# The last stage of a decoder on one core: norms in two VectorE passes, no GpSimd, weights prepared one stage earlier

## The chip, the cores and the metric

The kernel runs on 1 core of one Trainium2 chip. The metric is device time in microseconds (us) of one execution. The kernel before takes 4188.58 us, the median of 3 runs (4187.02 to 4195.04).

## The reference, cut to what matters

The network is a two-layer decoder: a recurrent mixer, cross attention, a mixture of experts, four selective-scan layers, an attention over feature maps, and at the end a quantised feed-forward network. Each sublayer is added to its input and layer-normalised. There are 4 batches of 512 tokens with 256 channels. Only the last sublayer is computed differently by the change:

```python
def act_quant_fake(x):
    scale = 127.0 / jnp.clip(jnp.max(jnp.abs(x), axis=-1, keepdims=True), 1e-05)
    return jnp.clip(jnp.round(x * scale), -128.0, 127.0) / scale
def weight_quant_fake(w):
    scale = 1.0 / jnp.clip(jnp.mean(jnp.abs(w)), 1e-05)
    return jnp.clip(jnp.round(w * scale), -1.0, 1.0) / scale
def bitlinear(x, w, b):
    return jnp.einsum('btd,hd->bth', act_quant_fake(x), weight_quant_fake(w)) + b
h = layernorm(x, ln1_g, ln1_b)        # 256 channels
h = bitlinear(h, w1, b1)              # 256 -> 1024
h = jax.nn.gelu(h, approximate=False)
h = layernorm(h, ln2_g, ln2_b)        # 1024 channels
h = bitlinear(h, w2, b2)              # 1024 -> 256
x = _layernorm(x + h)                 # what the kernel writes out
```

## The kernel before

The activations `x` stay in SBUF for the whole run as 128 partitions x 16 tiles x 256 channels; a batch is 4 tiles of 128 tokens (`TPB` = 4). Each sublayer is a stage of its own, a block with one written instruction stream for each engine, and a stage begins when all streams of the one before have ended. Inside a stage the engines are ordered by hand: a `Steps` object names the operations of one engine in their order, each completion adds one to a semaphore, and `wait_ge(*steps.at(name, turn))` holds an engine until that operation of that batch is done.

The last two compute stages are `feature_attention` (L2257) and `quantised_ffn` (L2536); `write_out` (L2846) follows.

**Attention stage.** Eight units `u` for each batch (4 tiles x 2 halves of the heads). TensorE makes scores, VectorE takes the row maximum (L2444), subtracts it (L2448), sums (L2438) and inverts (L2440) after ScalarE's exponential (L2369); GpSimd multiplies (L2327); TensorE transposes, ScalarE copies out (L2366); then come two products and, one batch later, the residual and norm. `head(b)` on VectorE (L2404) makes the block-diagonal operands from what ScalarE wrote in `projected(b)` (L2348).

**Quantised stage.** SyncE issues eight loads (L2585, L2589). VectorE sums the magnitudes of both weights (L2753), TensorE adds over partitions (L2787), VectorE scales and rounds the first weight in two passes (L2763, L2765), GpSimd the second (L2650, L2652), and ScalarE casts both to bf16 (L2598). Rounding is done by adding and taking away 1.5 * 2^23. For one batch of 4 tiles the chain is:

- first norm on VectorE: statistics (L221, L225, L228), ScalarE's root (L242), reciprocal (L233), subtract and multiply (L236), gain (L2696), offset (L2698);
- `quantise` on VectorE (L2663): maximum (L2669), three small operations (L2672, L2674, L2676), multiply and clip (L2679), clip and add the rounding constant (L2682), inverse scale (L2684); ScalarE takes the constant away into bf16 (L2607);
- TensorE transposes (L2795), ScalarE copies (L2610), TensorE multiplies into four PSUM banks (L2803), VectorE evacuates with scale and bias (L2708), ScalarE does the gelu (L2614);
- second norm over 1024 channels: statistics (L2715, L2719, L2722), root (L2618), reciprocal (L2726), subtract and multiply (L2729), gain (L2732) on VectorE, offset on GpSimd (L2657); then `quantise` again, ScalarE's cast (L2624), transposes (L2811), copies (L2628), the second product (L2817), and on VectorE the residual (L2741), the bias (L2745) and the last norm (L221 to L236 once more).

The order on VectorE is written by hand, with the first half of batch b+1 drawn between the parts of batch b:

```python
with v.Fori(0, B - 1) as b:
    first_stats(b + 1)
    second_norm(b)
    first_quantised(b + 1)
    second_quantised(b)
    first_products(b + 1)
    second_stats(b + 1)
    second_products(b)
```

`h2`, the hidden activations, has one buffer for all batches. `Fori` is a loop in the instruction stream with a register. The output leaves in one DMA of 2 MB after the last batch (L2852).

Of the kernel before, what the change touches and what calls it, by code (L numbers as in the profile page):

```python
# [2257 lines left out]
def feature_attention(nc, g, m):  # L2258
# [9 lines left out]
    with ExitStack() as ctx:  # L2268
# [31 lines left out]
        with nc.Block() as block:  # L2300
            @block.sync
            def _(sp):
# [5 lines left out]
                for dst, src in loads:  # L2308
                    sp.dma_start(dst, src).then_inc(weights_in, 16)
            n_loads = 16 * 6  # L2310
# [27 lines left out]
            def _(a):  # L2338
                begin(a, act_h, act_u, act_t)
# [56 lines left out]
            def _(v):  # L2396
                begin(v, dve_h, dve_u, dve_t)
# [35 lines left out]
                def body(b, tail=True):  # L2433
# [7 lines left out]
                    for u in us:  # L2441
# [9 lines left out]
                        if tail and u == 1:  # L2451
                            finish(b - 1)
                    sums(UN - 1)

                head(0)
                body(0, tail=False)
# [6 lines left out]
            def _(t):  # L2463
                begin(t, pe_h, pe_u, pe_t)
# [20 lines left out]
                def body(b, following=True):  # L2485
# [10 lines left out]
                    for u in us:  # L2496
# [6 lines left out]
                        if u >= LAG:  # L2503
                            at(u - LAG)
                        if following and u == 3:
                            transposes(b + 1)
                        if following and u == 7:
                            projections(b + 1)
# [17 lines left out]
                with t.Fori(0, B - 1) as b:  # L2526
                    body(b)
# [5 lines left out]
QUANT = " ".join(f"q{n}" for n in ["max", "clip", "rec", "scale"] + [f"{n}{q}" for n in ("mul", "low") for q in range(TPB)] + ["inv"])  # L2533


def quantised_ffn(nc, g, m):  # L2536
# [4 lines left out]
    HF = 1024  # L2541
    FC = HF // P
    with ExitStack() as ctx:
        sb, pb, sem = memory(nc, ctx)
        w1, w2 = sb("qf_w1", [P, DC, HF]), sb("qf_w2", [P, FC, D])
        wq1, wq2 = sb("qf_wq1", [P, DC, HF], BF16), sb("qf_wq2", [P, FC, D], BF16)
        wsum, wmean, wscale = sb("qf_wsum", [P, 2]), sb("qf_wmean", [P, 2]), sb("qf_wscale", [P, 2])
        identb = sb("qf_identb", [P, P], BF16)
        neground = sb("qf_neground", [P, 1])
# [4 lines left out]
        h2 = sb("qf_h2", [P, TPB, HF])  # L2554
        h2q = sb("qf_h2q", [P, TPB, HF], BF16)
        h2T = sb("qf_h2T", [P, TPB, FC, P], BF16)
# [6 lines left out]
        norm_in, w1_in, w2_in, rows_in = (sem(f"qf_{n}") for n in ("norm_in", "w1_in", "w2_in", "rows_in"))  # L2563

        ws, ws_g = Steps(sem("qf_weights_vector"), "ident sum mean clip rec r1 l1"), Steps(sem("qf_weights_pool"), "r2 l2")
        ws_a, ws_p = Steps(sem("qf_weights_scalar"), "q1 q2"), Steps(sem("qf_weights_tensor"), "sum")
        tl = range(TPB)
        each = lambda name: " ".join(f"{name}{q}" for q in tl)
        signal = lambda name, steps: Steps(sem(f"qf_{name}"), steps, 2)
        pre = lambda p, names: " ".join(p + n[2:] for n in names.split())  # L2570
        quant = lambda p: " ".join(p + n for n in QUANT.split())
        pe1, pe2 = signal("tensor_1", "h1T " + each("h")), signal("tensor_2", "h2T0 " + " ".join(f"h2T{q + 1} o{q}" for q in tl[:-1]) + f" o{TPB - 1}")
        act1, act2 = signal("scalar_1", "ansqrt q h1T " + each("g")), signal("scalar_2", "bnsqrt " + each("q") + " " + each("h2T") + " cnsqrt")
        dve1 = signal("vector_1", pre("an", LN_VECTOR) + " g1 b1n " + quant("a") + " " + each("e"))
        dve_st = signal("vector_stats", "bnstats bnmean bneps")
        dve2 = signal("vector_2", "bnrstd " + each("bnout") + " " + each("g2_") + " " + quant("b") + " res b2 " + pre("cn", LN_VECTOR))
# [3 lines left out]
        with nc.Block() as block:  # L2580
# [12 lines left out]
            def _(a):  # L2593
# [39 lines left out]
                for q in tl:  # L2633
                    gelu(0, q)
# [248 lines left out]
```

## Time and profile before

| what | value |
|---|---|
| median of 3 runs | 4188.58 us |
| the profiled execution, its own time | 4183.34 us |
| its span | 4181.5 us |
| busy in the span: TensorE, VectorE, ScalarE, GpSimd | 75%, 71%, 45%, 47% |
| chain that ended last | ends with the output DMA, then the last batch's norm |

The span is the time from the first to the last recorded instruction or transfer; the execution's own time has 1.84 us around it. The busy shares are means over all stages, and the change touches only what lies behind 3690 us, where the attention stage begins. Times in the profile are counted from the span's start. A timeline row gives the start, the busy time, the engine, the line, the operation, output and input, the count of instructions, and in brackets the idle time before them with what ended it. Rows of one kind that follow each other are merged.

### The profile page before, as it was taken

How to read it: one execution, taken by the hardware profiler on the slowest of the kernel's cores; microseconds unless marked ns; L12 is line 12 of the kernel's file. 1: busy time of each engine (PE TensorE's matmuls, PEld its weight loads, DVE VectorE, ACT ScalarE, POOL GpSimd, SP SyncE). 2: the span in 40 equal slices, each digit the busy share in tenths (PEclk: the TensorE clock that was granted, in tenths of full speed). 3: DMA queues.
4: the chain of work that ended last, by engine and by line, in shares of the span. 5: the costliest groups of instructions: out<-in, count | busy, mean ns of one | idle time of the engine just before them, and what ended most of it. 6: DMA issues, size and time to landing. Idle time of an engine off the chain costs nothing. (4 is left out here: it accounts for less than half of the span.)

```text
span 4181.5 us, 47419 instructions
## 1 busy us (share of the span) xinstructions
PE 3127.2 (75%) x16134; PEld 1728.5 (41%) x16134; DVE 2984.3 (71%) x3959; ACT 1885.0 (45%) x2885; POOL 1982.9 (47%) x1001
## 2 busy tenths in 40 slices
PE   6785888884664984788888988888998888657322
PEld 2234787774343751333333433333443333234111
DVE  2434666667541112899999999999999999946697
ACT  2323333321320113666667766666776666324232
POOL 0001111111213012678888878888878888722212
PEclk8775777776877996899999999999999999979665
DMA  1000000000021323343443444344444434300100
GB/s 39 0 0 6 0 0 0 0 0 5 18 87 60 114 89 103 111 149 137 156 144 132 148 138 157 133 147 142 153 139 139 146 134 141 131 13 0 39 0 20
DMA packets 120508, 342.10 MB, mean 82 GB/s; under 512 B 14667, under 2 KB 45602, under 8 KB 119618
## 3 DMA queue, kind: packets, MB, share of 16 engines
q1 hardware_dynamic: 114498, 332.01, 23.4%
q0 software_dynamic: 3072, 6.00, 0.7%
q10 hardware_dynamic: 2816, 2.62, 0.2%
q8 instruction: 57, 0.93, 0.1%
q14 instruction: 65, 0.53, 0.0%
HBM read 328.31 MB, written 14.68 MB: 82 GB/s over the span
## 5 line engine op out<-in xcount | busy, mean ns | idle before, releaser
L1916 POOL TENSOR_TENSOR mb_h<-mb_h,mb_BC 128x1024 f32<-128x1024 f32 x512 | 1212.2, 2384 | 362.1 <-DVE mb_h L2129 362.1
L2232 PE MATMUL mb_y<-mb_h,ident 128*128 128x512 f32 x2048 | 1027.6, 644 | 232.6 <-POOL mb_h L1916 231.1
L2129 DVE TENSOR_TENSOR_SCAN mb_h<-mb_dA,mb_bx 128x1024 f32<-128x1024 f32 x512 | 1170.6, 2286 | 17.8
L2034 ACT ACTIVATE mb_dA<-mb_delta,mb_A 128x511 f32<-128x511 f32 x1024 | 664.9, 712 | 415.6 <-DVE mb_h L2129 407.5
L2232 PEld LDWEIGHTS mb_y<-mb_h,ident 128*128 128x128 f32 x2048 | 399.0, 204 | 826.0 <-issue 429.8
L2125 DVE TENSOR_TENSOR mb_bx<-mb_du,mb_BC 128x1024 f32<-128x1024 f32 x512 | 630.2, 1231 | 72.4 <-ACT mb_du L1999 27.0
L254 PE MATMUL mb_p<-mb_xT,mb_in_w 128*128 128x512 f32 x512 | 237.3, 608 | 7.2 <-ACT mb_sz L1962 4.5
L254 PE MATMUL mb_p<-mb_upad,mb_convd 128*128 128x512 f32 x512 | 225.0, 592 | 0.8 <-ACT mb_upad L1950 0.8
L707 POOL COPY rs_vs<-rw_v 128x256 f32 x16 | 9.1, 568 | 446.1 <-PE rs_p L969 338.3
L1637 DVE TENSOR_TENSOR me_h<-me_s,me_p 128x320 f32<-128x320 f32 x64 | 31.2, 487 | 242.5 <-ACT me_s L1614 242.5
L846 DVE TENSOR_TENSOR rs_PQX<-rs_p,rs_PQX 128x128 f32<-128x128 f32 x320 | 85.7, 290 | 113.4 <-PE rs_p L946 112.4
L254 PEld LDWEIGHTS mb_p<-mb_xT,mb_in_w 128*128 128x128 f32 x512 | 98.6, 195 | 137.2 <-issue 118.6
L1591 POOL DMA_INDIRECT me_y<-expert_results,slot x32 | 31.0, 969 | 256.1 <-DMA expert_results<-me_oe 246.7
L254 PEld LDWEIGHTS mb_p<-mb_upad,mb_convd 128*128 128x128 f32 x512 | 96.8, 189 | 124.1 <-issue 124.1
L254 PE MATMUL me_p<-me_xeT,me_W 128*128 128x320 f32 x512 | 141.4, 437 | 0.9 <-ACT me_xeT L1602 0.9
L2034 ACT ACT_TABLE_LOAD x90 | 115.5, 1283 | 46.0 <-DVE mb_h L2129 44.7
L2657 POOL TENSOR_TENSOR qf_h<-qf_h,qf_b2n 128x1024 f32<-128x1024 f32 x16 | 50.1, 3160 | 163.1 <-DVE qf_h L2732 163.1
L749 ACT ACTIVATE rs_PQX<-rs_p 128x256 f32<-128x256 f32 x256 | 92.8, 382 | 70.6 <-PE rs_p L946 70.6
L343 POOL COPY rf_xs<-x 128x1024 f32 x4 | 4.2, 1038 | 237.3 <-PE rf_p L254 227.2
L254 PEld LDWEIGHTS me_p<-me_xeT,me_W 128*128 128x128 f32 x512 | 97.6, 192 | 43.6 <-issue 4.8
L254 PE MATMUL mb_p<-mb_out_w,mb_yg 128*128 128x256 f32 x512 | 113.2, 379 | 1.4 <-issue 1.4
L713 POOL TENSOR_TENSOR rs_Abd<-rs_Ac,rs_blockmask 128x512 f32<-128x512 f32 x64 | 80.9, 1265 | 66.5 <-DVE rs_Ac L838 66.3
(437 smaller groups left out, 5748.2 us busy)
## 6 DMA issues: line engine op xcount, KB each, us to landing
mb_BC<-mamba_BC SPq DMA_DIRECT2D x256, 1024.0 KB, 5.2
me_W<-in_L_ffn_W SPq DMA_DIRECT2D x24, 1024.0 KB, 9.1
mb_in_w<-in_L_attn_in_proj_w SPq DMA_DIRECT2D x4, 1024.0 KB, 8.2
mb_convd<-in_mamba_taps SPq DMA_DIRECT2D x4, 1024.0 KB, 10.2
expert_rows<-me_zero SPq DMA_DIRECT2D x1, 2560.0 KB, 10.1
x<-in_x SPq DMA_DIRECT2D x1, 2048.0 KB, 8.3
me_xe<-expert_rows SPq DMA_DIRECT2D x8, 256.0 KB, 10.7
expert_results<-me_oe ACTq DMA_DIRECT2D x8, 256.0 KB, 7.6
```

The source lines that it names most:

```text
L254: i = nc.tensor.matmul(out, lhsT, rhs, start=k == 0, stop=k == len(pairs) - 1)
L713: nc.gpsimd.tensor_tensor(Abd[h][:, :, :].rearrange("p m (q t) -> p m q t", q=NCH), Ac[h][:, :, :, :].rearrange("p x y (o t) -> p (x y) o ...
L749: nc.scalar.activation(PQX[h][:, 0:2 * P], bank[h][:, 0:2 * P], ACT.Copy).then_inc(*act(f"n{h}{k}"))
L846: nc.vector.tensor_tensor(X, bank[4 + h][:, 0:P], X, ALU.add).then_inc(*dve(f"x{h}{k}"))
L1591: nc.gpsimd.indirect_dma_start(out=y[:, k, i, :], out_offset=None, in_=outs, in_offset=idx(k, i)).then_inc(gathered[i // TPB], 16)
L1637: nc.vector.tensor_tensor(h[:, k, :], s1[:, k % 2, :], bank[3 + 2 * (k % 2)][:, 0:CAP], ALU.mult).then_inc(*dve(f"h{k}"))
L1916: tt(hk, hk, buffer(k, it)[:, 1, :, :], ALU.mult).then_inc(*pos(f"hc{k}{part}"))
L2034: i = av(dA[k % 2][:, c, s, 1:], delta[:, it % 2, mc, 1:], ACT.Exp, scale=A[:, MC * layer(it) + mc, n:n + 1])
L2125: tt(full(bx), du[c][:, :].rearrange("p (o t) -> p o t", o=1).broadcast_to([P, SU, T]), buffer(k, it)[:, 0, :, :], ALU.mult).then_inc(*dvs ...
L2129: nc.vector.tensor_tensor_scan(flat(h[k % NBUF][:, c, :, :]), flat(dA[k % 2][:, c, :, :]), flat(full(bx)), 0.0, ALU.mult, ALU.add).then_in ...
L2232: i = mm(ybank[c][:, :], m.ident[:, :], h[k % NBUF][:, c, s, :], start=False, stop=e == HALF - 1 and s == SU - 1)
L2657: nc.gpsimd.tensor_tensor(h2[:, q, :], h2[:, q, :], rows["b2n"][:, :], ALU.add).then_inc(*pool2(f"b2n{q}"))
```

## The change

- `tail_memory`: the weights' buffers and semaphores are made ahead of the attention stage. Both weight loads are issued by SyncE in that stage behind its own loads. VectorE sums the magnitudes between `head(0)` and the first batch's body, TensorE adds over partitions at unit 2 of batch 0, VectorE forms the mean at unit 5, rounds both weights in four passes after batch 0's body, and ScalarE casts both before batch 1. GpSimd does nothing for them.
- Each norm with gain and offset becomes two `scalar_tensor_tensor` passes on VectorE (`affine`): (x - mean) * gain, then * 1/sd + offset. GpSimd's offset pass is gone; the stage has no GpSimd work.
- Quantising: no clips. The first input takes one VectorE pass (multiply, add the rounding constant). The second takes one ScalarE pass with scale and bias; both keep ScalarE's pass that takes the constant away. The four maxima become one reduction (`largest`), and one small operation goes.
- `h2` has two buffers. All loops of the quantised stage and the first turn of TensorE's attention loop are written out. The order on all engines is new, and TensorE does all of batch b+1's first half ahead of batch b's second.
- Each batch's output leaves by a DMA of its own as soon as its last norm is done; `write_out` is gone.

```diff
+def weight_loads(sp, g, m):
+    for dst, name in ((m.w1, "ffn_w1_transposed"), (m.w2, "ffn_w2_transposed")):
+        sp.dma_start(full(dst), g[name].rearrange("(c p) n -> p c n", p=P)).then_inc(m.w_in, 16)
+def weight_sums(nc, v, m):
+    v.wait_ge(m.w_in, 32)
+    for k, w in enumerate((m.w1, m.w2)):
+        i = nc.vector.tensor_reduce(m.wsum[:, k:k + 1], w[:, :, :].rearrange("p c n -> p (c n)"), AX.X, ALU.add, apply_absolute_value=True)
+    i.then_inc(*m.ws("sum"))
+def weight_rounding(nc, v, m):
...
+    for k, w in enumerate((m.w1, m.w2)):
+        tsc(full(w), full(w), m.wscale[:, k:k + 1], 1.0, ALU.mult, ALU.min).then_inc(*m.ws(f"r{k + 1}"))
+    for k, w in enumerate((m.w1, m.w2)):
+        v.wait_ge(*m.ws.at(f"r{k + 1}"))
+        tsc(full(w), full(w), -1.0, ROUND, ALU.max, ALU.add).then_inc(*m.ws(f"l{k + 1}"))
+def weight_casts(nc, a, m):
+    for k, w, wq in ((1, m.w1, m.wq1), (2, m.w2, m.wq2)):
+        a.wait_ge(*m.ws.at(f"l{k}"))
+        nc.scalar.activation(full(wq), full(w), ACT.Identity, bias=m.round[:, 0:1]).then_inc(*m.ws_a(f"q{k}"))
 (feature_attention, ScalarE)
                 body(0, tail=False)
+                weight_casts(nc, a, m)
                 with a.Fori(1, B - 1) as b:
 (feature_attention, VectorE)
                 head(0)
-                body(0, tail=False)
+                weight_sums(nc, v, m)
+                body(0, tail=False, weights=True)
+                weight_rounding(nc, v, m)
 (quantised_ffn, SyncE)
+                for b in range(B):
+                    sp.wait_ge(*dve3.at("out", b))
+                    sp.dma_start(g["out"][b].rearrange("(t p) d -> p t d", p=P), tiles(b)).then_inc(x_out, 16)
 (quantised_ffn, ScalarE; av = nc.scalar.activation)
+                def second_half(b):
+                    a.wait_ge(*dve2.at("rec", b))
                     for q in tl:
+                        av(h2[:, b % 2, q, :], h2[:, b % 2, q, :], ACT.Identity, scale=q2["scale"][:, q:q + 1], bias=m.round[:, 1:2]).then_inc(*act3(f"r{q}"))
+                    for q in tl:
+                        a.wait_ge(*act3.at(f"r{q}", b))
                         a.wait_ge(*pe2.at(f"h2T{q}", b - 1))
+                        av(h2q[:, q, :], h2[:, b % 2, q, :], ACT.Identity, bias=m.round[:, 0:1]).then_inc(*act3(f"q{q}"))
+                for b in range(B):
+                    if b + 1 < B:
+                        first_sqrt(b + 1)
                     second_sqrt(b)
+                    if b:
+                        last_sqrt(b - 1)
+                    if b + 1 < B:
+                        first_half(b + 1)
+                        gelu(b + 1)
+                    second_half(b)
 (quantised_ffn, VectorE)
+                def affine(dve, j, src, h, mean, inverse, gain, offset):
+                    v.wait_ge(*dve.at("rstd", j))
                     for q in tl:
+                        stt(h(q), src(q), mean[:, q, 0:1], gain, ALU.subtract, ALU.mult).then_inc(*dve(f"g{q}"))
+                    for q in tl:
+                        v.wait_ge(*dve.at(f"g{q}", j))
+                        stt(h(q), h(q), inverse[:, q:q + 1], offset, ALU.mult, ALU.add).then_inc(*dve(f"n{q}"))
+                def largest(dve, j, h, sc):
+                    v.wait_ge(*dve.at(f"n{TPB - 1}", j))
+                    nc.vector.tensor_reduce(sc["max"][:, :], h, AX.X, ALU.max, apply_absolute_value=True).then_inc(*dve("max"))
...
+                for b in range(B):
+                    if b + 1 < B:
+                        first_stats(b + 1)
+                    second_stats(b)
+                    if b:
+                        second_products(b - 1)
                     second_norm(b)
+                    if b:
+                        last_norm(b - 1)
+                    if b + 1 < B:
+                        first_quantised(b + 1)
+                    second_largest(b)
+                    if b + 1 < B:
+                        first_products(b + 1)
                 second_products(B - 1)
+                last_norm(B - 1)
```

## Rows read from the trace of the kernel before

**Rows 1.** The page, busy time of each engine, its share and its instructions.
```profile
PE 3127.2 (75%) x16134; PEld 1728.5 (41%) x16134; DVE 2984.3 (71%) x3959; ACT 1885.0 (45%) x2885; POOL 1982.9 (47%) x1001
```
**Rows 2.** Windows: length; busy PE, PEld, DVE, ACT, POOL; clock; DMA share; GB/s.
```profile
4005.50:4063.00 57.50, 15.57 (x94) 8.68 (x91) 52.83 (x99) 18.94 (x21) 12.56 (x4) 0.58 0.00 0
...
4119.40:4173.40 54.00, 11.01 (x92) 8.26 (x89) 36.54 (x76) 13.90 (x17) 12.42 (x4) 0.62 0.00 0
```
**Rows 3.** Groups of instructions, quantised stage: busy, mean ns of one, idle before.
```profile
L2657 POOL TENSOR_TENSOR qf_h<-qf_h,qf_b2n 128x1024 f32<-128x1024 f32 x16 | 50.1, 3160 | 163.1 <-DVE qf_h L2732 163.1
L236 DVE TENSOR_SCALAR qf_h<-x,qf_lna_mv,qf_lna_rstd 128x256 f32 (+1 forms) x16 | 35.7, 2292 | 0.1
...
L2708 DVE SCALAR_TENSOR_TENSOR qf_h<-qf_p,qf_inv,qf_b 128x512 f32<-128x512 f32 x32 | 22.1, 745 | 13.1 <-PE qf_p L254 11.5 <-ACT qf_h2T L2628 1.5
...
L236 DVE TENSOR_SCALAR x<-x,qf_lnc_mv,qf_lnc_rstd (+1 forms) x16 | 5.5, 408 | 0.1
```
**Rows 4.** Timeline, start of the quantised stage: a load, and both weights' passes.
```profile
3905.77 0.43 SPq L2585 DMA_DIRECT2D qf_b1n<-in_L_ffn_ln_b  x1
...
3919.87 1.29 DVE L2763 TENSOR_SCALAR qf_w<-qf_w,qf_wscale 128x2048 f32<-128x2048 f32 x1
3919.94 8.24 POOL L2650 TENSOR_SCALAR qf_w<-qf_w,qf_wscale 128x2048 f32<-128x2048 f32 x1 [40.48 <-DVE qf_wscale L2760]
3921.19 8.07 DVE L2765 TENSOR_SCALAR qf_w<-qf_w 128x2048 f32<-128x2048 f32 x1
```
**Rows 5.** Timeline of VectorE, quantised stage, where each part of a batch starts.
```profile
4018.28 1.40 DVE L221 BATCH_NORM_STATS2 qf_lna_stats<-x 128x6 f32 x4
...
4020.36 0.18 DVE L2726 RECIPROCAL qf_rstd<-qf_sd 128x4 f32<-128x4 f32 x1
...
4062.93 4.83 DVE L2715 BATCH_NORM_STATS2 qf_stats<-qf_h 128x6 f32<-128x512 f32 x8
...
4068.69 1.66 DVE L2741 SCALAR_TENSOR_TENSOR x<-qf_o,qf_inv,x 128x256 f32 x4
...
4074.16 0.18 DVE L233 RECIPROCAL qf_lnc_rstd<-qf_lnc_sd 128x4 f32<-128x4 f32 x1 [0.27 <-ACT qf_lnc_sd L242]
```
**Rows 6.** Timeline of VectorE, batch 0: the end of quantising, and the first evacuation.
```profile
3943.80 0.22 DVE L2684 TENSOR_SCALAR qf_inv<-qf_max,qf_wmean 128x4 f32<-128x4 f32 x1
3949.75 5.52 DVE L2708 SCALAR_TENSOR_TENSOR qf_h<-qf_p,qf_inv,qf_b 128x512 f32<-128x512 f32 x8 [5.73 <-PE qf_p L254]
```
**Rows 7.** Timeline, last batch: first cast, first residual, output.
```profile
4154.66 4.27 ACT L2624 ACTIVATE qf_h2q<-qf_h,qf_neground 128x1024 bf16<-128x1024 f32 x4 [23.50 <-DVE qf_h L2682]
...
4166.28 1.66 DVE L2741 SCALAR_TENSOR_TENSOR x<-qf_o,qf_inv,x 128x256 f32<-128x256 f32 x4 [9.71 <-PE qf_o L254]
...
4173.62 0.39 SPq L2852 DMA_DIRECT2D out_x<-x  x1
```
**Rows 8.** Groups by form, whole kernel, VectorE: prices of the new passes.
```profile
L800 DVE SCALAR_TENSOR_TENSOR rs_right<-rs_Em,rw_kk 128x1024 f32<-128x1024 f32 x16 | 19.5, 1218 | 0.0
...
L2753 DVE TENSOR_REDUCE qf_wsum<-qf_w 128x1 f32<-128x2048 f32 x2 | 4.6, 2286 | 5.9 <-DMA qf_w<-in_ffn_w_transposed 5.9
```
**Rows 9.** Timeline of the attention stage, batches 0 and 1: where the weight work goes.
```profile
3723.36 0.69 DVE L2444 TENSOR_REDUCE fa_mx<-fa_p 128x8 f32<-128x512 f32 x1 [3.28 <-PE fa_p L254]
...
3742.93 2.04 POOL L2327 TENSOR_TENSOR fa_A<-fa_E,fa_sm 128x512 f32<-128x512 f32 x2 [1.12 <-DVE fa_sm L2440]
...
3755.44 2.50 DVE L2411 TENSOR_TENSOR fa_Kbd<-fa_kf,fa_hmask 128x512 f32<-128x512 f32 x4 [11.25 <-ACT fa_qf L2355]
...
3764.50 0.63 ACT L2369 ACTIVATE fa_E<-fa_E 128x512 f32<-128x512 f32 x1 [8.49 <-DVE fa_E L2448]
```
**Rows 10.** DMA issues, last two stages: KB each, us from issue to landing.
```profile
fa_fcT<-in_feature_out SPq DMA_DIRECT2D x1, 512.0 KB, 3.9
...
qf_b1n<-in_L_ffn_ln_b SPq DMA_DIRECT2D x1, 128.0 KB, 4.8
```
**Rows 11.** Waits, first 700 us: who waited for whom, us in total, times, longest.
```profile
DVE rf_xT L358 <- issue: 1.9, 1, 1.9
```

More of the change, by code:

```diff
@@ L2525, in _ @@
                 projections(0)
-                with t.Fori(0, B - 1) as b:
+                body(0, weights=True)
+                with t.Fori(1, B - 1) as b:
                     body(b)
@@ L2532, with tail_memory @@
 ROUND = 1.5 * 2.0 ** 23
-QUANT = " ".join(f"q{n}" for n in ["max", "clip", "rec", "scale"] + [f"{n}{q}" for n in ("mul", "low") for q in range(TPB)] + ["inv"])
+HF, FC2 = 1024, 1024 // P
+def tail_memory(nc, ctx, m):
+    sb, pb, sem = memory(nc, ctx)
+    m.w1, m.w2 = sb("qf_w1", [P, DC, HF]), sb("qf_w2", [P, FC2, D])
+    m.wq1, m.wq2 = sb("qf_wq1", [P, DC, HF], BF16), sb("qf_wq2", [P, FC2, D], BF16)
+    m.wsum, m.wmean, m.wscale = sb("qf_wsum", [P, 2]), sb("qf_wmean", [P, 2]), sb("qf_wscale", [P, 2])
+    m.round = sb("qf_round", [P, 2])
+    m.w_in = sem("qf_w_in")
+    m.ws = Steps(sem("qf_weights_vector"), "sum mean clip rec r1 r2 l1 l2")
+    m.ws_a, m.ws_p = Steps(sem("qf_weights_scalar"), "q1 q2"), Steps(sem("qf_weights_tensor"), "sum")
@@ new lines, in weight_loads, with weight_total @@
+def weight_loads(sp, g, m):
[6 more added lines that the diff above has]
+    i.then_inc(*m.ws("sum"))
+def weight_total(nc, t, m, out):
+    t.wait_ge(*m.ws.at("sum"))
+    nc.tensor.matmul(out, m.ones[:, :], m.wsum[:, :], start=True, stop=True).then_inc(*m.ws_p("sum"))
@@ L2692, in first_quantised @@
                 def first_quantised(j):
+                    v.wait_ge(*act1.at("sqrt", j))
+                    nc.vector.reciprocal(lna.rstd[:, :], lna.sd[:, :]).then_inc(*dve1("rstd"))
                     v.wait_ge(*act1.at("q", j - 1))
[L2694 to L2697 removed]
@@ new lines, in second_product @@
+                    t.wait_ge(*dve3.at("res", b - 1))
+                    product(nc, obank[q // 2][:, (q % 2) * D:(q % 2 + 1) * D], [(h2T[:, q, c, :], m.wq2[:, c, :]) for c in range(FC2)]).then_inc(*pe2(f"o{q}"))
+                t.wait_ge(ident_made, 1)
+                t.wait_ge(*m.ws_a.at("q2"))
+                for b in range(-1, B):
+                    if b + 1 < B:
+                        transposes(b + 1)
+                        for q in tl:
+                            first_product(b + 1, q)
+                    if b >= 0:
+                        second_transposes(b, 0)
+                        for q in tl:
+                            if q + 1 < TPB:
+                                second_transposes(b, q + 1)
+                            second_product(b, q)
```

339 lines of the change are left out of this document (141 added, 198 removed).

## The prediction

> **What bounds the kernel now.** I read the page first. No engine is busy all the time, and its shares [rows 1] are means over stages that the change does not touch. The diff touches the attention stage, in which it adds work, and the quantised stage, from 3905 us to the end at 4181.5: 276 us, 6.6% of the span. No more than that can be won.
>
> Second, the windows of the quantised stage [rows 2]. In a middle batch VectorE is busy 52.8 of 57.5 us, ScalarE 18.9, TensorE 15.6, GpSimd 12.6: VectorE bounds it. In the last batch it is busy 36.5 of 54.0: there is no next batch to fill its waits, and the chain through the engines sets the time.
>
> Third, the groups of that stage [rows 3]. The reader is to see two rows of one line: L236 on 128x256 takes 408 ns in the last norm and 2292 ns in the first. In the timeline the same shows with the weights [rows 4]: a pass over 128x2048 takes 1.29 us (L2763), the next takes 8.07 us (L2765), and that is how long GpSimd's pass (L2650, 8.24 us) still runs. So VectorE passes of this kind stand still beside GpSimd, and a part of "busy" is waiting. The slow L236 passes fall where GpSimd adds the offset (L2657).
>
> **Prices of the parts of VectorE's new order.** First statistics 2.1 us (4018.28 to 4020.36), second statistics 5.8 (4062.93 to 4068.69), residual, bias and last statistics 5.2 (4068.69 to 4074.16 less the 0.27 wait) [rows 5]. Evacuation 5.5 [rows 6]. Last norm: four passes of 408 ns that overlap a little, and a reciprocal of 0.2: 1.6 [rows 3, 5].
>
> Not shown is the fused pass with two SBUF inputs and a per-partition scalar. At 1024 elements the nearest row is L800, 1.22 alone [rows 8]; between 1.14 (it overlaps its neighbour) and 1.31 (a pointer scalar costs it more) I take 1.2. The second norm is then 8 x 1.2 + 0.2 = 9.8. At 256 elements L2741 does four in 1.66 [rows 5], so eight take 3.3. Reductions: 2048 elements take 2.29 [rows 8], so 1024 take 1.2 and 4096 take 4.5. First norm with quantising: 0.2 + 3.3 + 1.2 + 0.4 (two small operations) + 1.4 (four passes like the 408 ns one) = 6.5, and 0.2 for the inverse scale. The second maximum with its small operations is 5.1; the scale that ScalarE waits for is there after 4.9. In sum a middle batch has 2.1 + 5.8 + 5.2 + 9.8 + 1.6 + 6.7 + 5.1 + 5.5 = 41.8 us of VectorE, where it had 52.8 in 57.5.
>
> **Which wait ends last then.** From the last quantising pass to the first evacuation there are 5.95 us of cast, transposes, copy and product on ScalarE and TensorE (3943.80 to 3949.75) [rows 6]. From ScalarE's first cast of the second half to the residual there are 11.6 (4154.66 to 4166.28) [rows 7]. ScalarE's new rounding pass stands ahead of that: not shown as such, but a pass of its form takes 4.27 for four [rows 7], so 4.2; bounds 4.0, and 4.9 if the second pointer costs.
>
> ScalarE does all gelus of batch b+1 before the second half of batch b. The gelus end 1.1 after VectorE's last evacuation (call this moment T). So the residual of batch b can start only at T + 1.1 + 4.2 + 11.6 = T + 16.9. VectorE has but 2.1 + 5.8 = 7.9 us of work until then: 9.0 us of new idle time in each of three batches. That is what is late next, and why I don't count the whole 52.8 - 41.8 with the old waits as gain.
>
> **The sum on VectorE's clock.**
> - Start: the first norm no longer waits for weights but for its offset row, issued at 3905.77 [rows 4] and landed 4.8 later [rows 10]: 3910.6. Statistics are done before. + 6.5 + 5.95 + 5.5: T0 = 3928.6. Before, this was 3949.75 + 5.52 = 3955.3: 26.7 won.
> - Batch 0's second half: 7.9 + 0.3 for the root, + 9.8 + 6.5 + 5.95 + 5.5 = 35.9. The maximum (5.1) hides in the 5.95. T1 = 3964.5.
> - Two middle turns: 16.9 + 5.2 + 9.8 + 1.6 + 6.5 + 5.95 + 5.5 = 51.45 each (57.5 before): T3 = 4067.4.
> - Last: 16.9 + 5.2 + 9.8 + 1.6 = 33.5; scale at + 4.9; ScalarE and TensorE 4.2 + 11.6; then from the residual to the output's issue 7.3 as before (4166.28 to 4173.62) [rows 7]: 61.5. The output of the last batch is issued at 4128.9, 44.7 earlier than now.
> - Output: three batches leave beside other work, 1.5 MB in three 50 us turns. 2 MB took 7.9 from issue to the span's end [rows 7]; the last 512 KB should take 4.3 (a load of 512 KB lands in 3.9 [rows 10], plus issuing). 3.6 won.
>
> **What moves into the attention stage.** SyncE issues two loads more behind its own eight; nobody waits for SyncE, and the loads have some 15 us until VectorE wants them. VectorE's two sums (4.6 [rows 8]) stand ahead of the first row maximum, where it idles 3.28 for TensorE [rows 9]: 1.3 late, nearly all taken up by the next wait for TensorE. TensorE's small product and the mean are under 1. The four rounding passes (4 x 1.29, [rows 4], with small operations some 6) stand ahead of `vz` and `Kbd` of batch 1, where VectorE idles 11.25; ScalarE's two casts (4.0) stand where it idles 8.49 [rows 9]. If these covers failed, 4.6 + 0.8 + 6 + 4 = 15 would show; from below, nothing is removed from this stage, so no gain. I take 0.5, as the covers are wide.
>
> Rounding meets GpSimd's last two products of batch 0, which end at 3744.97 (3742.93 + 2.04) [rows 9]; VectorE's first pass would be ready at about 3744.3, so VectorE waits, inside its cover, and the sum stands. The Trainium skill (SBUF — State Buffer, Who interferes with whom) has a rule that speaks against this place: whichever of the two engines issues first holds the shared port pair for its whole instruction, and the other blocks. By that rule, if GpSimd comes later than VectorE, a pass of 1.3 us holds up GpSimd, and the products wait; the trace agrees that a blocked pass waits for the whole other instruction [rows 4], and the sum would be 1.3 to 5 more.
>
> **Total.** Start to issue 44.7 + output 3.6 - 0.5 = 47.8. The profiled execution is 4183.34 (span 4181.5 and 1.84 around it), so it would be 4135.5. The median shown is 5.2 above it; against that median: 4188.58 - 47.8 = 4140.8, which I give as 4141.
>
> **The rivals.**
> - *VectorE never idles.* If ScalarE and TensorE got the second half through in the 7.9 us, each of three batches would save 9.0: 4114. For it: the windows show those engines mostly idle. Against it: the last batch's chain is a latency (9.71 idle before the residual [rows 7]), and the gelus stand ahead of it by the written order. 7%.
> - *The covers in the attention stage fail*, by the port collision or because TensorE's chain takes the delay on: up to 10 of the 15, so 4151. The rule above is this rival's. 13%.
> - *The slowness of L236 is not GpSimd's doing*, and the first norm stays slow whatever form it has: 7.9 in each of three turns and 6.6 at the start, 30 in all: 4171. Against it: the same line is fast in every place without GpSimd. 5%.
> - *The change's last word, loops written out, costs code loading.* Place: TensorE, ScalarE and VectorE each run three more written bodies of the quantised stage. Price: the one VectorE wait in the first 700 us that nothing explains is 1.9 [rows 11]; nine of them are 17: 4158. It decides the sign only above 48 / 9 = 5.3 each; then the kernel is slower than before. 7%, of which 2% past that point.
> - My forecast: 68%.
>
> **How the numbers follow.** About 0.2% is what a measurement of this kernel can tell from no change, so faster means below 4180. All but the far ends of the last two rivals are below: faster 0.95, same 0.03, slower 0.02. The range: downwards the fused passes at 1.14 (32 of them, 2 us), a quicker landing of rows and output (3), and the runs' scatter (4 to either side): 4131, and a little toward the second case, 4129. Upwards 4 for fused passes and ScalarE, 10 for the attention stage, some code loading: 4158.
>
> **What the changed profile would show.** L236's 2292 ns rows are gone, and no GpSimd row stands in the quantised stage. In the windows a middle batch takes 51 with VectorE busy 41 to 42. Before the residuals of the first three batches VectorE idles about 9 us on TensorE's `qf_o`, and before the last one 15 to 16. Fused 1024 passes at 1.2. The attention stage keeps its length within 1 us, and its ScalarE wait of 8.49 shrinks to about 4.5. I am wrong if that residual wait is missing (then it is 4114), if the attention stage has grown by several us, or if rows wait on "issue" in the written-out bodies.

## The result, and the profile after

The kernel after takes 4143.3 us (median of 4 runs, 4140.46 to 4144.29), the kernel before beside it 4190.44 (4 runs, 4187.02 to 4195.04): a ratio of 0.9883, 95% interval 0.987 to 0.9895. That is 47.1 us less at the median. The forecast was 4141, 47.8 less than the 4188.58 that the kernel before had then.

The profiled execution is 4140.46 with a span of 4138.6. From profile to profile 42.9 us of span are gone, and three stretches make that up. The cuts are the end of the last L236 pass of the stage ahead of the attention stage, the end of the attention stage's last L236 pass, and the end of the span.

| stretch | before | after | forecast | measured |
|---|---|---|---|---|
| all up to the attention stage (not touched) | 3696.13 | 3702.97 | 0 | +6.84 |
| attention stage | 208.98 | 209.19 | +0.5 | +0.21 |
| quantised stage | 276.39 | 226.44 | -48.3 | -49.95 |

The first line is not the change. In the ten experiments below, whose code is the same up to there, this point lies between 3702.15 and 3711.25; the profile of before is the early end of that scatter. From here on experiments are compared by the length of the quantised stage, which begins behind it. Each length comes from one profile. How far such a length scatters can be read from the attention stage: in the nine profiles that have the weights' work in it, it takes 208.3 to 209.3, without that work 208.8 to 209.1. So a difference below about 1 us says nothing, and the +0.21 of the attention stage is one of these.

The busy row of the page of the kernel after, which answers to [rows 1]:

```profile
PE 3137.5 (76%) x16131; PEld 1737.7 (42%) x16134; DVE 2928.8 (71%) x3890; ACT 1902.6 (46%) x2899; POOL 1916.9 (46%) x983
```

VectorE lost 55.5 us of busy time and its share is the same 71%. The page's first row can't tell that anything was won. The windows can. First batch's start, middle turn, and last turn of the quantised stage, after (columns as in [rows 2]):

```profile
3916.10:3933.90 17.80, 6.75 (x23) 2.56 (x24) 11.76 (x26) 6.62 (x6) 0.00 (x0) 0.59 0.24 86
3968.80:4020.50 51.70, 15.64 (x87) 9.70 (x88) 39.66 (x80) 22.01 (x23) 0.00 (x0) 0.64 0.03 11
...
4072.90:4135.30 62.40, 17.48 (x128) 13.20 (x128) 32.51 (x64) 28.11 (x29) 0.00 (x0) 0.62 0.03 9
```

A middle turn had 52.83 of VectorE in 57.50 [rows 2]; now it has 39.66 in 51.70. VectorE's busy time fell by 13.2 us, of which 7.9 were L236 standing still beside GpSimd (its four passes took 9.26 there; they take 1.38 in the run without GpSimd below). The turn fell by only 5.8. Where the rest went stands in the timeline of VectorE, after, batch 1's turn (each row: start, busy, engine, line, operation, names, shapes, count, idle before):

```profile
3970.61 4.84 DVE L2777 BATCH_NORM_STATS2 qf_stats<-qf_h 128x6 f32<-128x512 f32 x8
...
3987.07 1.66 DVE L2802 SCALAR_TENSOR_TENSOR x<-qf_o,qf_inv,x 128x256 f32<-128x256 f32 x4 [10.96 <-PE qf_o L254]
...
3992.16 4.87 DVE L2737 SCALAR_TENSOR_TENSOR qf_h<-qf_h,qf_mv,qf_g 128x1024 f32<-128x1024 f32 x4
3996.96 4.87 DVE L2740 SCALAR_TENSOR_TENSOR qf_h<-qf_h,qf_rstd,qf_b2n 128x1024 f32<-128x1024 f32 x4
...
4009.53 0.23 DVE L2760 TENSOR_SCALAR qf_inv<-qf_max,qf_wmean 128x4 f32<-128x4 f32 x1
4009.66 4.41 DVE L2744 TENSOR_REDUCE qf_max<-qf_h 128x4 f32<-128x4096 f32 x1
...
4014.99 5.50 DVE L2769 SCALAR_TENSOR_TENSOR qf_h<-qf_p,qf_inv,qf_b 128x512 f32<-128x512 f32 x8 [0.38 <-issue]
```

VectorE stands idle 10.96 us before the residual, on TensorE's second product. In all four batches that is 51.0 us, by the waits of VectorE, after:

```profile
DVE x L2802 <- PE qf_o L254: 51.0, 4, 16.6
DVE qf_h L2769 <- PE qf_p L254: 6.5, 5, 5.5
```

The chain behind that wait, ScalarE and then TensorE, after, same turn:

```profile
3969.76 4.62 ACT L2688 ACTIVATE qf_h<-qf_h,qf_round,qf_scale 128x1024 f32<-128x1024 f32 x4
3974.29 4.25 ACT L2692 ACTIVATE qf_h2q<-qf_h,qf_round 128x1024 bf16<-128x1024 f32 x4
```

```profile
3979.50 1.89 PE L254 MATMUL qf_o<-qf_wq,qf_h2T 128*128 128x256 bf16 x8 [1.95 <-ACT qf_h2T L2696]
...
3982.03 1.91 PE L254 MATMUL qf_o<-qf_wq,qf_h2T 128*128 128x256 bf16 x8
...
3984.59 2.37 PE L254 MATMUL qf_o<-qf_wq,qf_h2T 128*128 128x256 bf16 x16
```

The start of the stage, on VectorE, after: the offset row is the last to arrive, for 0.85 us, and the four first passes of the norm, 2292 ns each in before [rows 3], are four fused ones in 1.67 us.

```profile
3916.06 0.18 DVE L2752 RECIPROCAL qf_lna_rstd<-qf_lna_sd 128x4 f32<-128x4 f32 x1 [0.85 <-DMA qf_b1n<-in_L_ffn_ln_b]
3916.35 1.67 DVE L2737 SCALAR_TENSOR_TENSOR qf_h<-x,qf_lna_mv,qf_g 128x256 f32<-128x256 f32 x4
...
3928.07 2.95 DVE L2769 SCALAR_TENSOR_TENSOR qf_h<-qf_p,qf_inv,qf_b 128x512 f32<-128x512 f32 x4 [5.48 <-PE qf_p L254]
```

And the attention stage, after: the weights' sums and rounding on VectorE, and the casts on ScalarE, which answer to [rows 9].

```profile
3727.08 4.47 DVE L2567 TENSOR_REDUCE qf_wsum<-qf_w 128x1 f32<-128x2048 f32 x2
...
3751.34 3.02 DVE L2591 TENSOR_SCALAR qf_w<-qf_w,qf_wscale 128x2048 f32<-128x2048 f32 x2
3754.28 2.35 DVE L2594 TENSOR_SCALAR qf_w<-qf_w 128x2048 f32<-128x2048 f32 x2
...
3762.40 2.50 DVE L2413 TENSOR_TENSOR fa_Kbd<-fa_kf,fa_hmask 128x512 f32<-128x512 f32 x4 [5.44 <-ACT fa_qf L2356]
```

```profile
3750.03 2.05 POOL L2328 TENSOR_TENSOR fa_A<-fa_E,fa_sm 128x512 f32<-128x512 f32 x2 [1.09 <-DVE fa_sm L2442]
```

```profile
3762.78 3.98 ACT L2600 ACTIVATE qf_wq<-qf_w,qf_round 128x2048 bf16<-128x2048 f32 x2
...
3771.46 0.63 ACT L2370 ACTIVATE fa_E<-fa_E 128x512 f32<-128x512 f32 x1 [4.71 <-DVE fa_E L2450]
```

The idle time before `Kbd` fell from 11.25 to 5.44 and ScalarE's from 8.49 to 4.71: the added work lies in them.

### The profile page after: what moved, and what is told of

It reads as the page before. It is cut to its first block and busy times, and to the rows that moved or that the text cites. A ratio compares the mean times of both kernels' runs of the same rounds, so it can differ in the third digit from the quotient of the medians.

```text
span 4138.6 us, 46982 instructions
## 1 busy us (share of the span) xinstructions
PE 3137.5 (76%) x16131; PEld 1737.7 (42%) x16134; DVE 2928.8 (71%) x3890; ACT 1902.6 (46%) x2899; POOL 1916.9 (46%) x983
## 5 line engine op out<-in xcount | busy, mean ns | idle before, releaser
L2129 DVE TENSOR_TENSOR_SCAN mb_h<-mb_dA,mb_bx 128x1024 f32<-128x1024 f32 x512 | 1170.6, 2286 | 17.8
L254 PEld LDWEIGHTS mb_p<-mb_out_w,mb_yg 128*128 128x128 f32 x512 | 97.2, 190 | 21.8 <-issue 9.4
## 6 DMA issues: line engine op xcount, KB each, us to landing
me_xe<-expert_rows SPq DMA_DIRECT2D x8, 256.0 KB, 10.7
```

Of the source, the lines that this page charges most:

```text
L254: i = nc.tensor.matmul(out, lhsT, rhs, start=k == 0, stop=k == len(pairs) - 1)
L2129: nc.vector.tensor_tensor_scan(flat(h[k % NBUF][:, c, :, :]), flat(dA[k % 2][:, c, :, :]), flat(full(bx)), 0.0, ALU.mult, ALU.add).then_in ...
```

## The experiments

The theory has three parts. GpSimd's passes held VectorE's up, and with the weights' work ahead of the first norm they cost the most. The new turn is bound by the written order on ScalarE and TensorE; on ScalarE it puts the rounding pass and the casts of batch b behind all gelus of batch b+1. Pass counts and the output's tail count only where nothing else is waited for. Against it: the slow passes had another cause, or the order costs nothing because VectorE is late anyway, or written-out loops change the time by themselves.

All results in one table; the stage is the quantised one, from the profiled run. The kernel before ran beside the experiments: its medians were 4192.19 (13 runs) beside the table's first three and the rounding on VectorE, 4191.43 (7) beside the other three on order, 4188.71 (7) beside three passes and one output, 4190.51 (6) beside both parts.

| kernel | median (range), runs | ratio to before, 95% | stage |
|---|---|---|---|
| before without GpSimd | 4170.81 (4168.37 to 4176.95), 4 | 0.9944, 0.9928 to 0.9961 | 254.97 |
| before, weights moved | 4168.76 (4167.42 to 4173.24), 4 | 0.9945, 0.9928 to 0.9961 | 250.94 |
| before, loops written out | 4192.31 (4189.69 to 4197.26), 10 | 0.9999, 0.9989 to 1.0008 | 275.47 |
| before, both parts | 4154.35 (4151.41 to 4160.57), 4 | 0.9915, 0.9897 to 0.9933 | 238.36 |
| after, rounding on VectorE | 4132.63 (4131.93 to 4138.55), 4 | 0.9859, 0.9843 to 0.9876 | 216.23 |
| after, casts first | 4136.71 (4134.31 to 4141.47), 4 | 0.9862, 0.9846 to 0.9879 | 219.71 |
| after, interleaved order | 4133.37 (4133.22 to 4133.89), 4 | 0.9857, 0.984 to 0.9873 | 215.84 |
| after, interleaved, rounding on VectorE | 4113.54 (4112.85 to 4114.89), 4 | 0.981, 0.9794 to 0.9826 | 199.35 |
| after, three-pass norms | 4152.73 (4144.58 to 4156.24), 4 | 0.9912, 0.9896 to 0.9929 | 239.23 |
| after, one output | 4146.29 (4141.41 to 4150.33), 4 | 0.9898, 0.9882 to 0.9915 | 231.03 |

**Before without GpSimd.** The offset pass and the second weight's rounding go to VectorE; nothing else moves.

```diff
 (quantised_ffn, GpSimd: nothing left; VectorE)
+                    for q in tl:
+                        v.wait_ge(*dve2.at(f"g2_{q}", b))
+                        tt(h2[:, q, :], h2[:, q, :], rows["b2n"][:, :], ALU.add).then_inc(*pool2(f"b2n{q}"))
...
+                tsc(full(w2), full(w2), wscale[:, 1:2], 1.0, ALU.mult, ALU.min).then_inc(*ws_g("r2"))
+                v.wait_ge(*ws_g.at("r2"))
+                tsc(full(w2), full(w2), -1.0, ROUND, ALU.max, ALU.add).then_inc(*ws_g("l2"))
```

> The kernel before with the four GpSimd offset passes of each batch and GpSimd's two weight passes given to VectorE, nothing else. Theory (VectorE stands still beside GpSimd): L236 of the first norm falls from 2292 to about 410 ns; each middle turn loses 7.9 us of standing still and gains 4.6 of adds, the start wins some 11; the quantised stage goes from 276.4 to about 256, the time to about 4170. Rival (the first norm is slow by itself): L236 keeps its 2292 ns, VectorE only gets work, the stage grows to about 290, the time to about 4204.

The stage is 21.4 us shorter although VectorE does more. Groups of VectorE in the quantised stage, this kernel:

```profile
L2725 DVE TENSOR_TENSOR qf_h<-qf_h,qf_b2n 128x1024 f32<-128x1024 f32 x16 | 18.5, 1218 | 0.0
...
L236 DVE TENSOR_SCALAR qf_h<-x,qf_lna_mv,qf_lna_rstd 128x256 f32 (+1 forms) x16 | 5.5, 409 | 0.1
```

The first norm's L236 passes take 409 ns where they took 2292 [rows 3], by the same line and on the same data. And the second weight pass, 8.07 us beside GpSimd [rows 4], is back at its own price. VectorE's timeline, same kernel:

```profile
3934.98 1.29 DVE L2756 TENSOR_SCALAR qf_w<-qf_w,qf_wscale 128x2048 f32<-128x2048 f32 x1
3936.30 1.23 DVE L2758 TENSOR_SCALAR qf_w<-qf_w 128x2048 f32<-128x2048 f32 x1
```

The slowness was GpSimd's doing: the rival in which it had another cause falls.

**Before with the weights moved.** The loads, sums, rounding and casts of the weights stand in the attention stage as in the change; all else is as before, with GpSimd's offset pass in place.

```diff
+                weight_loads(sp, g, m)
...
+                weight_sums(nc, v, m)
+                body(0, tail=False, weights=True)
+                weight_rounding(nc, v, m)
...
+                weight_casts(nc, a, m)
```

> The kernel before with only the weight work moved into the attention stage, as the change does it. Theory (wide covers): the attention stage keeps its length within 0.5 us, the first evacuation of batch 0 ends 25 us earlier, the quantised stage goes from 276.4 to about 251, the time to about 4165. Rival (the covers fail): the attention stage is longer by up to 15 us, and the time falls only to about 4175 to 4180.

25.4 us of stage are gone, and the attention stage takes 209.31 against 208.98. The first norm, on VectorE's timeline of this kernel, waits for its offset row as in the kernel after and is fast even in its old form, as no weight pass runs on GpSimd beside it:

```profile
3918.74 0.18 DVE L233 RECIPROCAL qf_lna_rstd<-qf_lna_sd 128x4 f32<-128x4 f32 x1 [0.95 <-DMA qf_b1n<-in_L_ffn_ln_b]
3918.95 1.38 DVE L236 TENSOR_SCALAR qf_h<-x,qf_lna_mv,qf_lna_rstd 128x256 f32<-128x256 f32 x4
```

**Before with its loops written out.** The counterpart of the code-loading rival.

```diff
-                with a.Fori(0, B - 1) as b:
+                for b in range(B - 1):
 (the same for the loops of GpSimd, VectorE and TensorE)
```

> The kernel before with only the four loops of the quantised stage written out, same order, same waits. Theory (loops cost next to nothing, written code neither): the quantised stage stays at 276.4 within 1.5 us, the time within the scatter of the kernel before, 4187 to 4195. Rival (code loading costs): unexplained waits on the engines in the written bodies, the stage 5 to 17 us longer. Second rival (the loops themselves cost): the stage 3 us shorter or more.

The ratio is 0.9999, the stage 275.47 against 276.39. Writing out the loops neither costs nor gains anything that can be measured here.

**Before with both parts.** The weights moved and the offset pass on VectorE: the diff of the weights moved, and the offset pass of the run without GpSimd.

> The kernel before with two parts of the change together: the weights' work in the attention stage, and GpSimd's offset pass on VectorE, so that the quantised stage has no GpSimd work. Clips, three-pass norms, loops, the interleaved order and the one output stay as before. My theory: both parts act through the same block at the stage's start, so their single gains (25.4 and 21.4 us) do not add. The start is that of the run with the weights moved (23.2 us from the stage's start to the last evacuation of batch 0), the turns are those of the run without GpSimd (47.3, 53.0, 53.5) and its end (61.9): 238.9 us of quantised stage, 37.5 less than before, time about 4153 against 4191. The other parts of the change (fused passes, quantising, order, output by batch) are then worth 12.5 us together. Rival: the two gains add in full: stage 229.6, time 4144, and the rest of the change is worth 3.

Stage 238.36, that is 38.0 less than before where the single gains add to 46.8: the block at the start belonged to both. It leaves 11.9 us between this kernel and the kernel after for all the rest: fused passes, quantising, order and outputs. The next experiments undo these one at a time.

**After with three-pass norms.**

```diff
-                        stt(h(q), src(q), mean[:, q, 0:1], gain, ALU.subtract, ALU.mult).then_inc(*dve(f"g{q}"))
+                        tsc(h(q), src(q), mean[:, q, 0:1], inverse[:, q:q + 1], ALU.subtract, ALU.mult).then_inc(*dve(f"s{q}"))
+                    for q in tl:
+                        v.wait_ge(*dve.at(f"s{q}", j))
+                        tt(h(q), h(q), gain, ALU.mult).then_inc(*dve(f"g{q}"))
...
-                        stt(h(q), h(q), inverse[:, q:q + 1], offset, ALU.mult, ALU.add).then_inc(*dve(f"n{q}"))
+                        tt(h(q), h(q), offset, ALU.add).then_inc(*dve(f"n{q}"))
```

> The kernel after, but each norm with gain and offset in three VectorE passes (subtract and multiply by 1/sd; times gain; plus offset) in place of two fused ones. My theory: the count of passes is on VectorE's path, behind the wait before the residual. At 1024 channels a tensor_scalar pass for four tiles should be about 3.0 us and the two others 4.6 each, 12.2 where the fused pair takes 9.65: 2.6 more for each batch. The first norm over 256 channels should be 0.9 longer. Four batches: 14 us, so the quantised stage takes about 240 (226.4 in the kernel after) and the time is about 4157. Rival: the overlap of neighbouring passes makes their count nearly irrelevant; then the stage stays within 3 us of 226.4 and the time is 4143 to 4146.

The stage is 12.8 us longer. VectorE's timeline of this kernel, second norm of batch 2:

```profile
4049.14 2.98 DVE L2737 TENSOR_SCALAR qf_h<-qf_h,qf_mv,qf_rstd 128x1024 f32<-128x1024 f32 x4
4052.04 4.62 DVE L2740 TENSOR_TENSOR qf_h<-qf_h,qf_g 128x1024 f32<-128x1024 f32 x4
4056.58 4.62 DVE L2743 TENSOR_TENSOR qf_h<-qf_h,qf_b2n 128x1024 f32<-128x1024 f32 x4
```

The first pass costs 0.75 us a tile and each of the others 1.16; the fused passes cost 1.22 each. So "three passes into two" is worth 2.4 us for four tiles here and not a third: the pass saved is the cheap one. The Trainium skill (VectorE: DVE Perf Modes, Mode 2×_2P) says that an operation with one tensor input can read it through both ports at twice the rate in fp32, and one with two tensor inputs can't. These rows agree, as far as a step from 1.16 to 0.75 with its fixed part can show it.

**After with one output.** The four DMAs of 512 KB become one of 2 MB after the last norm.

```diff
-                for b in range(B):
-                    sp.wait_ge(*dve3.at("out", b))
-                    sp.dma_start(g["out"][b].rearrange("(t p) d -> p t d", p=P), tiles(b)).then_inc(x_out, 16)
+                sp.wait_ge(*dve3.at("out", B - 1))
+                sp.dma_start(g["out"].rearrange("b (t p) d -> p (b t) d", p=P), full(m.x)).then_inc(x_out, 16)
```

> The kernel after, but with one output transfer of 2 MB after the last batch in place of one for each batch. My theory: the transfers of the first three batches lie beside other work for nothing, and only what follows the last norm counts: from the end of the last norm to the end of the span about 7.9 us (8.15 in the kernel before, 3.36 in the kernel after), so the quantised stage takes about 231 us and the time is about 4148. Rival: the early transfers slow VectorE or the chain beside them by as much as they save at the end; then the turns between the batches get shorter by 1 to 1.5 us each, the stage stays at 226 to 227, and the time is 4143.

The output is issued at 4137.90 of a span of 4145.8, so 7.9 us stand behind it; in the kernel after it is 3.3. The stage is 4.6 longer, all of it there. From median to median the kernel after is 3.0 us faster; against the kernel before that ran beside each, 42.4 us are won here and 47.1 there, which is 4.7 apart. The two intervals of the ratio overlap, so the tail is shown by the trace and not by the times alone.

**After with the rounding of the second input on VectorE.** One `tensor_scalar` pass per tile, ahead of the first evacuation, in place of ScalarE's.

```diff
-                        av(h2[:, b % 2, q, :], h2[:, b % 2, q, :], ACT.Identity, scale=q2["scale"][:, q:q + 1], bias=m.round[:, 1:2]).then_inc(*act3(f"r{q}"))
 (ScalarE)
...
+                    v.wait_ge(*dve2.at("rec", b))
+                    for q in tl:
+                        tsc(h2[:, b % 2, q, :], h2[:, b % 2, q, :], q2["scale"][:, q:q + 1], ROUND, ALU.mult, ALU.add).then_inc(*dve2(f"low{q}"))
 (VectorE)
```

> The changed kernel with ScalarE's rounding pass of the second input given back to VectorE, as one pass over each tile (four of about 0.7 us). Theory (ScalarE's and TensorE's chain behind the gelus sets the residual): ScalarE's chain is 4.5 us shorter, VectorE's 2.7 longer; each residual comes 2.2 us earlier after the scale, the last one 3.8; the quantised stage goes from 226.4 to about 216, the time to about 4133. Rival (VectorE's own work bounds the turns): each turn is 2.7 longer, the stage about 234, the time about 4151.

10.2 us of stage less, by giving work back to the engine that was called the bound. VectorE's waits in the stage, this kernel:

```profile
DVE x L2801 <- PE qf_o L254: 29.9, 4, 10.0
```

The wait before the residual fell from 51.0 to 29.9, which is 21.1, and VectorE took on 4 x 2.74 = 11.0 of work: the difference is the gain. So one part of the change, the rounding on ScalarE, made the kernel slower. The Trainium skill (ScalarE: Activation LUTs, Rules for kernel authors) says to do additions and multiplications on VectorE rather than ScalarE. Here four tiles take 4.62 on ScalarE and 2.74 on VectorE, so the trace agrees; what decides is on which side of the wait the pass stands.

**After with the casts ahead of the gelus.** Only ScalarE's order changes: rounding and casts of batch b, then gelus of batch b+1, then the copies of batch b.

```diff
-                        gelu(b + 1)
...
+                    if b + 1 < B:
+                        gelu(b + 1)
+                    second_copies(b)
```

> The changed kernel with one change of order on ScalarE: rounding and casting of batch b ahead of the gelus of batch b+1, the copies out of PSUM behind them. Theory: ScalarE starts the rounding at the scale, 6 us before VectorE's last evacuation, but the gelus (with their table load) then stand ahead of the copies, and from the first copy to the residual there are still 8.6 us of TensorE and ScalarE taking turns: each of three residuals comes only about 2 us earlier, the stage goes to about 221, the time to about 4138. Rival (the casts alone are what is late): residuals 6 to 8 us earlier, stage about 205, time about 4122.

6.7 us of stage less, by ScalarE's order alone. VectorE's waits, this kernel: part of the wait moved to the gelus, which now come late for the second statistics.

```profile
DVE x L2806 <- PE qf_o L254: 32.7, 4, 16.5
DVE qf_stats L2781 <- ACT qf_h L2679: 11.2, 3, 5.2
```

**After in the interleaved order.** ScalarE does the gelu of tile q behind the copy of tile q of batch b, and TensorE draws the second half of batch b between the products of batch b+1, as the kernel before does.

```diff
 (ScalarE, second_half)
+                        if b + 1 < B:
+                            gelu(b + 1, [q])
 (TensorE; each line stands for its waits and products)
+                        first_product(b + 1, 0)
+                        first_product(b + 1, 1)
+                        second_transposes(b, 0)
+                        second_transposes(b, 1)
+                        first_product(b + 1, 2)
+                        second_product(b, 0)
...
```

> The changed kernel with the orders of the kernel before on ScalarE (each copy of batch b followed by a gelu of batch b+1) and on TensorE (second half of batch b drawn between the first products of b+1); the rounding stays on ScalarE. Theory (the idle time before the residual is made by the written order): residual 19 to 20 us behind the scale instead of 24.4, though TensorE's later first products now hold up VectorE's evacuation; three times 4.9: the stage about 212, the time about 4129. Rival (the held-up evacuation eats it): no gain, 4143 within 3.

10.6 us of stage less, 4 short of what was expected. The waits before the first three residuals are gone, only the one before the last residual stays, and a new wait took part of their place: VectorE now waits for the first product, because TensorE's written order puts the transposes of batch b ahead of the third product of batch b+1, and these transposes wait for ScalarE's rounding and casts. Waits of VectorE, this kernel:

```profile
DVE qf_h L2770 <- PE qf_p L254: 29.1, 9, 6.2
DVE x L2803 <- PE qf_o L254: 16.9, 1, 16.9
```

**Both: interleaved, rounding on VectorE.** The two diffs together.

> The changed kernel with both: rounding of the second input on VectorE, and the interleaved orders of the kernel before on ScalarE and TensorE. Theory: ScalarE casts 0.8 us behind the scale and needs 13.3 us from there to the last product, as the trace of before shows; the residual comes about 15.4 us behind the scale instead of 24.4 in three turns, and the last 3.8 earlier: the stage about 196, the time about 4112. Rival (the gains of the two don't add, VectorE's 2.7 more and its wait for TensorE return most): about 4128, like the interleaving alone.

The stage takes 199.35 (3 more than expected) and the kernel 4113.54, which beats both: 0.981 of before, with an interval of 0.9794 to 0.9826 that does not touch that of the kernel after. Waits of VectorE, and the window of a middle turn, this kernel:

```profile
DVE qf_h L2767 <- PE qf_p L254: 10.4, 5, 5.5
DVE x L2802 <- PE qf_o L254: 9.9, 1, 9.9
```

```profile
3971.90:4016.50 44.60, 12.47 (x90) 7.28 (x90) 42.32 (x85) 17.22 (x20) 0.00 (x0) 0.66 0.04 12
```

VectorE is busy 95% of the turn, against 77% in the kernel after, and the turn takes 44.6 where it took 51.7. Only the last batch, which has no next batch's work to fill its wait, still waits before its residual. Together the two edits gain 27.1, more than 10.2 + 10.6: each takes away the wait that limited the other. That reading is argued from the two lists of waits; no run separates it further.

## Why the prediction was right

The steps on VectorE's clock, counted from the start of the stage (T0 to T3 are the ends of the four batches' evacuations):

| step | forecast | measured |
|---|---|---|
| stage start to T0 | 23.5 | 21.8 |
| T0 to T1 | 35.9 | 34.8 |
| T1 to T2, T2 to T3 | 51.45 each | 51.7, 52.4 |
| T3 to the output's issue | 61.5 | 62.4 |
| issue to the end | 4.3 | 3.3 |
| sum | 228.1 | 226.4 |

**The mechanism held.** The slow passes are gone with GpSimd, and the run without GpSimd shows that this was the cause. The wait that ends last is the one named, TensorE's product before the residual, in each batch. The chain behind it sets it, as the runs show that reorder or shorten that chain: ScalarE's order alone is worth 6.7, ScalarE's and TensorE's together 10.6, the rounding taken off ScalarE 10.2. The turn is therefore 51.7 and not the 42 of the forecast's VectorE work. That work itself was 39.7, as most of its parts were a little shorter than their prices.

**The terms that were off** are five, and they partly cancel. The four residuals started later than forecast by 1.4, 1.4, 0.9 and 0.9 us, 4.6 in all; everything else in the sum came out 6.3 shorter. That the stage is within 1.7 of its forecast is in part luck.

- The chain from the first cast to the residual: forecast 11.6, measured 12.78 (3974.29 to 3987.07). The last batch of before, from which it was taken, had TensorE at the upper clock for the second half of it. In the middle turn of after TensorE is at the lower level (granted 0.50) for longer:

```profile
3979.40:3983.20 3.80, 3.70 (x22) 2.91 (x23) 0.00 (x0) 1.87 (x3) 0.00 (x0) 0.50 0.00 0
3983.20:3987.10 3.90, 3.77 (x28) 2.82 (x26) 0.03 (x1) 2.35 (x3) 0.00 (x0) 0.72 0.00 0
3984.00:3985.00 1.00, 1.00 (x10) 0.90 (x9) 0.00 (x0) 0.16 (x1) 0.00 (x0) 0.50 0.00 0
```

  and that of before, in the same part of its last batch:

```profile
4160.00:4163.00 3.00, 3.00 (x21) 2.41 (x21) 0.00 (x0) 1.07 (x2) 0.00 (x0) 0.56 0.00 0
4163.00:4166.30 3.30, 2.92 (x30) 2.19 (x27) 0.02 (x1) 1.71 (x2) 0.00 (x0) 1.00 0.00 0
```

  The row that starts at 3984.00 shows that the clock is still at the lower level up to 10.7 us after the first cast. A product of one tile takes 1.89 at 1.2 GHz and 1.05 at 2.4. Before its first transposes TensorE had stood idle 8.25 us here, and 32.38 in before, where the clock rose sooner; so in these two places the shorter idle time did not bring the earlier rise.
- ScalarE's rounding: taken at 4.2 between bounds of 4.0 and 4.9, measured 4.62, and 4.53 from its start to the first cast. With the chain it puts the residual 18.3 behind the end of the last evacuation and not 16.9 (17.8 in the third batch). The idle time before it is 10.96 and not 9.0, as VectorE's two statistics take 7.4 and not 7.9. In the third batch it is 12.43: no next batch follows whose first statistics could fill it. The forecast's 9.0 "in each of three batches" missed that; its sum, which goes by 16.9, did not.
- Against it, last quantising pass to first evacuation: 5.95 forecast, 5.45 to 5.7 measured. Why it is shorter was not tested.
- The offset row landed 3.2 us after its issue and not 4.8. It is the second load of the stage in every kernel. In the three profiles with the two weight loads of 1 MB each issued right behind it (before, without GpSimd, loops written out) it took 4.8 to 4.9, in the nine others 3.1 to 3.5; the run with only the weights moved has 3.2. So these loads held it up.
- The output's tail: 3.3, not 4.3. A 512 KB transfer out ended sooner than the 512 KB load that it was priced by.

**The fused passes**, a price that no row showed, were right: 4.87 for four at 1024 elements (1.22 each) for 1.2 taken, and 1.67 for four at 256 for 1.66. Undone, the expectation was 14 us and the run gave 12.8.

**The attention stage** took 0.2 for 0.5. The first rounding pass was ready at 3751.34 and met the last two GpSimd products, which end at 3752.08; the pair of passes took 3.02 where two by themselves take 2.5 (1.29 and 1.28 in the run without GpSimd, where they stand apart). So VectorE waited about 0.5 and GpSimd was held up by nothing, as its two products take 2.05 for 2.04 [rows 9]. The collision went the way in which it stays within the cover, and so it did in all nine profiles with the weights' work here: 3.02 for the pair, 2.04 to 2.05 for the products. The other way, in which a VectorE pass holds up these products, no run shows. And 0.2 is inside the 1 us by which this stage scatters, so the runs show a cost near nothing and not its size.

**One reading of the rows** was a little off: the weight pass of 8.07 us ends at 3929.26, but GpSimd's at 3928.18 [rows 4]. It stood still for 7.0 and then took its own 1.1, close to the 1.23 that it takes without GpSimd.

**The profiled time** is 5.0 above the 4135.5 of the sum: +6.84 of scatter ahead of the attention stage, -1.65 in the quantised stage, -0.3 in the attention stage. At the median, where the scatter averages out, 47.1 was won of 47.8.

**The rivals.** VectorE never idling (4114) did not happen in this kernel. That the last experiment ends at 4113.54 is no proof of that rival's price: its first three residual waits are gone, but VectorE has 11.0 us more work, its waits for the first product grew by 3.9, and the last residual wait is 6.7 shorter. That these add up to the same number is chance. The covers held. GpSimd as the cause is shown. Written-out loops cost nothing.

**The parts of the change, as the runs give them** in the quantised stage: weights moved 25.4; GpSimd's offset pass on VectorE a further 12.6; all the rest 11.9. In that rest two passes for three are worth 12.8 and the output by batch 4.6, while the order on ScalarE and TensorE costs 10.6. By subtraction 5.1 remain for the one maximum, the clips left out, VectorE's new order and the rounding on ScalarE together. That is an estimate that holds only if the parts add, and order and rounding do not (27.1 together, 10.2 and 10.6 alone). What the maximum and the clips are worth was not measured.

## What to carry to other kernels

When work is taken off the busiest engine, ask at once what it will wait for: here 13 us of VectorE's busy time left a turn and 6 us of time did, because a written order put one batch's chain behind another batch's gelus. A pass moved to a less busy engine is no gain if that engine stands on the chain that ends last; moving it back to the "bound" engine, into its idle time, was worth 10 us. And where a pass is several times slower in one place than in another by the same line, as L236 was here, look at what GpSimd does beside it before costing anything by its mean.

## What the runs showed of the hardware

- Code that is the same up to 3700 us ended there between 3696.13 and 3711.25 in twelve profiled runs. Stages of the same runs agree far better: the attention stage took 208.3 to 209.3 in all. A change of 15 us at the end could not be read from two spans alone.
- VectorE's passes over 128x256 with one tensor input took 409 ns with GpSimd still and 2292 beside its 3.16 us passes, by the same line.
- ScalarE needs 4.62 us for four 128x1024 passes with scale and bias both read from memory, and 4.25 with the bias alone and a bf16 output: 0.09 a pass more. No run separates the second pointer from the output type.
- TensorE rose from 1.2 to 2.4 GHz at different points of the same chain of work: granted 1.00 from 8.3 us after the first cast in the last batch of before, but still 0.50 up to 10.7 us after it in a middle turn of after.
- A load of 128 KB landed 4.8 to 4.9 us after its issue with two loads of 1 MB issued right behind it (three profiles), and 3.1 to 3.5 without them (nine profiles).
